# A fused vision tower on one core: the value product of each four tiles is issued one slot later

## The chip, the cores and the metric

The kernel runs on one core of a Trainium2 chip. The metric is the device time of one execution in microseconds (us); lower is better. TensorE (PE) multiplies matrices, ScalarE (ACT) applies functions such as exp, VectorE (DVE) reduces and adds, GpSimd (POOL) does small elementwise work, SyncE (SP) issues the transfers. Each engine runs its own instructions strictly in the order in which they were written, and waits at a semaphore until another engine has raised it.

## What is computed

A batch of 16 items of 1024 tokens of 64 features passes through a patch embedding, two attentions with 8 heads of 8 features, and two expert networks. Nearly all of the time goes into the attentions:

```python
qkv = (x @ qkv_w.T).reshape(B, N, 3, H, D).transpose(2, 0, 3, 1, 4)
q, k, v = (qkv[0], qkv[1], qkv[2])
attn = jnp.einsum('bhnd,bhmd->bhnm', q, k) * scale
attn = jax.nn.softmax(attn, axis=-1)
out = jnp.einsum('bhnm,bhmd->bhnd', attn, v)
```

N is 1024 and H is 8. The first attention adds a bias; between and after the attentions stand layer norms, projections, a two-layer routed network and a top-2 expert network with gelu.

## The kernel before

**Tiles and slots.** The scores of one item and one attention are cut into 128 tiles of 128 keys by 512 queries; with 16 items and two attentions there are 4096 tiles. The program runs through *slots*, one for each tile n. The attentions of two items are interleaved with everything else in a *pair* of 256 slots. There are 15 pairs, 12 of them in a loop, with a phase of 128 slots ahead and one behind. In what follows a slot is named by its number in the pair, 0 to 255.

**The work of a slot.** TensorE issues in slot n, in this order: the side stages put there by hand (layer norm transposes, projections, expert layers; these are all lines but the three named here); the *score product* of tile n (line 914, `scores`), which puts 128x512 scores into one of three PSUM banks, the ring; and a *natural product* (line 902, `nat`) for a tile 46 slots ahead, of which VectorE takes the row maxima (line 1322). ScalarE then turns the scores into `prob` with exp (line 1113), which frees the bank. Once in four slots comes the *value product* (line 928, `pv`): it multiplies `prob` of four tiles by the values, four heads side by side in the array, and adds them up in the bank `acc`.

**What a score product waits for.** The ring of three banks is planned at build time (`score_ring`). A tile normally gets the bank of the tile three before it, and so waits for exp(n-3). A side stage that needs a bank of the ring takes it and keeps it for four tiles (`SIDE_TILES`); during those four slots the tiles alternate between the other two banks, and tile n waits for exp(n-2). I call these *two-bank* slots. The plan has some 1300 of them, in runs of four, so that about 330 fall on each remainder of n by four. In slots with n % 4 of 0 or 1 that are two-bank, the natural product is issued ahead of the score product (`scores_first`); in all others the score product comes first.

**What the value product waits for.** `pv` of tiles 4k to 4k+3 waits for exp(4k+3), line 927. The first one of a half item also waits until ScalarE has copied the finished `acc` out (line 1094, `acc_out`, after the exp of each slot that is 2 modulo 64), and that copy in turn waits for the value product before. `prob` has 8 buffers; exp(4k) waits for the value product of tiles 4k-8 to 4k-5.

**The expert network.** In slot 50 of each pair stands `FW`: on TensorE eight steps of four products each (lines 855 and 857), and on ScalarE eight gelu of 128x1024 (line 1085) behind a load of its function table. Its first step waits for the mask, its second step for the exp of slot 49, and from the third step on TensorE and ScalarE take turns. The line 871 follows in slot 51.

Of the kernel before, what the change touches and what calls it, by code (L numbers as in the profile page):

```python
# [49 lines left out]
HEADS = 4  # L50
# [275 lines left out]
def super_of(kind, it, q):  # L326

    n = q // SUPERS
    if kind == "first":
        a, b = 0, n  # L330
    elif kind == "last":
        a, b = 1, B - 1 + n
    elif n == 0:
        a, b = 0, it + 1
    elif n == 1:
        a, b = 1, it
    else:
        a, b = (1, B - 1) if isinstance(it, int) and it == B - 2 else (0, it + 2)
    return a, b, q % 2, q % SUPERS // 2


def max_tiles(side, n):


    def extra(m):
        for slot in range(m, max(m - 3 * AHEAD, -1), -1):
            if any(x[0] == "FW" for x in side.get(slot, ())):
                return AHEAD - (m - slot) // 3
        return 0

    return range(n + SUPER + LEAD + (extra(n - 1) if n else 0), n + SUPER + LEAD + extra(n) + 1)


def before_phase(kind, it):

    if kind == "first":
        return None
    if kind == "last":
        return 1, B - 2
    return (0, 0) if isinstance(it, int) and it == 0 else (1, it - 1)  # L360


def tower_kernel(nc, x, w_dft, dft, const, onehot, qk_w, v_w, pw, qk_scale, wi, routed, shared, wo, bo,
                 table, route, wg, w1, b2, w2, out):
    with ExitStack() as ctx:
# [142 lines left out]
        def n_tiles(kind):  # L508

            return 2 * ATTN if kind == "pair" else ATTN  # L510
# [186 lines left out]
        def _(eng):  # L697
# [185 lines left out]
            def turn(n0, q, n):  # L883

                eng.wait_ge(parts_ready, over(n0, SUPER) + q + 1)
                eng.matmul(side_bank(n, 1)[:, 0:P], mpart[:, q % 2, :], ident_b[:, :], start=True, stop=True)\
                    .then_inc(side_full[1], 1)

            def nat(kind, it, n0, m):
                q, j = m // SUPER, m % SUPER  # L890
                a, b, g, half = super_of(kind, it, q)
                u = buffer_of(a, b)
                if q % SUPERS == 0 and j == 0:
                    if a == 0 and b < 2:
                        eng.wait_ge(s_rows[u], 2 * PARTS * 16)
                    eng.wait_ge(qk_in[u][0], at(DMA_QK * (loads_before(a, b) + 1)))
                if q % SUPERS == 1 and j == 0:
                    eng.wait_ge(qk_in[u][1], at(DMA_QK * (loads_before(a, b) + 1)))
                use = n0 + m
                eng.wait_ge(nat_free, at(use - len(NAT) + 1))  # L900
                h, c, kh = HEADS * g + j // 8, half * 512 + j % 8 // 2 * P, j % 2
                eng.matmul(NAT[use % len(NAT)][:, :], QA[u][0:K_NAT, h, c:c + P],  # L902
                           KA[u][0:K_NAT, h, kh * 512:kh * 512 + 512], start=True, stop=True)\
                    .then_inc(nat_ready, 1)

            def scores(kind, it, n0, n):
                q, i = n // SUPER, n % SUPER
                a, b, g, half = super_of(kind, it, q)
                u = buffer_of(a, b)
                if i == 0:  # L910
                    eng.wait_ge(maxrow_in[q % 2], at(DMA_MAX * (over(n0, 2 * SUPER) + q // 2 + 1)))
                bank_wait(TILE_PREV[n0 + n])
                t, h = i // HEADS, HEADS * g + i % HEADS
                eng.matmul(RING[TILE_BANK[n0 + n]][:, :], KA[u][0:K_ALL, h, t * P:t * P + P],  # L914
                           QA[u][0:K_ALL, h, half * 512:half * 512 + 512], start=True, stop=True)\
                    .then_inc(st_ready, 1)

            def pv(a, b, g, n0, first_tile):

                t = first_tile % SUPER // HEADS  # L920
                q = first_tile // SUPER
                if t == 0 and g == 0:
                    eng.wait_ge(acc_free, at(over(n0, 2 * SUPER) + q // 2))
                    if q % SUPERS == 0:
                        eng.wait_ge(vc_done, at(vc_index(a, b)))
                eng.wait_ge(exp_done, at(n0 + first_tile + HEADS))
                for hh in range(HEADS):
                    mm = eng.matmul(ACC[32 * hh:32 * hh + 32, :], VZ[buffer_of(a, b)][:, t, HEADS * g + hh, :],  # L928
                                    prob[:, (first_tile + hh) % TILES, :],
                                    start=(t == 0 and g == 0), stop=(t == JT - 1 and g == 1),  # L930
                                    skip_group_check=True)
                mm.then_inc(pv_done, 1)

            def body(kind, it, n0, side, found):
                if kind == "serial":
                    for k, stage in enumerate(side):
                        side_stage(stage, found[0, k], N_TILES, 0)
                    return
                if kind == "first":
                    eng.wait_ge(s_dve, SET_DVE)  # L940
                    eng.wait_ge(s_pool, SET_POOL)
                    for m in range(SUPER + LEAD):
                        if m == SUPER + LEAD - SUPER + TURN:
                            turn(n0, 0, found[-1, 0])
                        nat(kind, it, n0, m)
                for n in range(n_tiles(kind)):
                    if kind == "first" and n == LATE:
                        eng.wait_ge(s_rest, N_SET[s_rest])
                    tiles = max_tiles(side, n)
                    between = [(kind, it, n0, m) for m in tiles[:-1]]  # L950
                    for k, stage in enumerate(side[n]):
                        if stage[0] == "TN":
                            turn(n0, stage[1], found[n, k])
                        else:
                            side_stage(stage, found[n, k], n0 + n, n, between)
                    two_banks = TILE_PREV[n0 + n] == ("tile", n0 + n - 2)
                    scores_first = n % HEADS >= 2 or not two_banks
                    if scores_first:
                        scores(kind, it, n0, n)
                    for m in tiles[len(between):]:  # L960
                        if kind != "last" or m < ATTN:
                            nat(kind, it, n0, m)
                    if not scores_first:
                        scores(kind, it, n0, n)
                    if n % HEADS == 1 and n > 1:
                        done = n - 1 - HEADS
                        a, b, g, _ = super_of(kind, it, done // SUPER)
                        pv(a, b, g, n0, done)
                    elif n == 1 and kind != "first":
                        pv(*before_phase(kind, it), 1, n0, -HEADS)  # L970
                if kind == "last":
                    a, b, g, _ = super_of(kind, it, SUPERS - 1)
                    pv(a, b, g, n0, ATTN - HEADS)

            run_phases(eng, reg, body)


# [607 lines left out]
```

## Time and profile before

| what | value |
|---|---|
| median of 3 runs | 3964.97 us (3964.28 to 3965.2) |
| the profiled execution | 3963.26 us |
| its span, first to last instruction | 3961.5 us |
| mean granted TensorE clock | 0.985 of full speed |
| TensorE busy | 3796.0 us, 96% |
| VectorE busy | 2913.7 us, 74% |
| ScalarE busy | 2588.0 us, 65% |
| GpSimd busy | 873.0 us, 22% |

A matmul is shown as busy until its result has drained, some 0.38 us for 512 columns, while the next one starts after 0.22 us. So a wait of TensorE shows as idle time only for the part beyond that overlap, and the distance from start to start of two rows tells more than the busy share.

### The profile page before, as it was taken

What the parts mean: (1) busy time and instruction counts of PE and PEld (TensorE: products, weight loads), DVE (VectorE), ACT (ScalarE), POOL (GpSimd) and SP (SyncE); (2) the same over time, 40 slices, a digit from 0 to 9 for tenths busy, and PEclk for the clock granted to TensorE, in tenths of its full rate; (3) what the DMA queues carried; (4) which work ended last, traced back from release to release, by engine and by line L of the source; (5) the groups of instructions that cost most, each with busy time, mean ns of one, the idle gap of its engine ahead of it and who ended that gap; (6) DMA issues with size and microseconds to landing.
All of it is one profiled execution on the core that took longest, in us unless ns stands there. A gap on an engine that the chain in (4) does not pass through costs nothing.

```text
span 3961.5 us, 62513 instructions
## 1 busy us (share of the span) xinstructions
PE 3796.0 (96%) x21508; PEld 1325.7 (33%) x21508; DVE 2913.7 (74%) x5001; ACT 2588.0 (65%) x4720; POOL 873.0 (22%) x1265
## 2 busy tenths in 40 slices
PE   6999999999999999999999999999999999999896
PEld 3233333333333333333333333333333333333332
DVE  4877868677786877868677786877868678787672
ACT  0566667666676666766667676676666667677564
POOL 4122212132221312212122121312212122121211
PEclk7899999999999999999999999999999999999998
DMA  5213201212121122201212112122211222111100
GB/s 108 40 26 67 44 20 33 59 37 44 35 43 38 33 47 49 43 22 33 57 39 44 32 42 42 33 47 49 39 26 33 55 41 44 31 30 33 21 13 6
DMA packets 119068, 156.37 MB, mean 39 GB/s; under 512 B 24847, under 2 KB 66575, under 8 KB 118717
## 3 DMA queue, kind: packets, MB, share of 16 engines
q1 hardware_dynamic: 118753, 152.38, 19.2%
q8 instruction: 172, 2.82, 0.3%
q14 instruction: 143, 1.17, 0.1%
HBM read 120.01 MB, written 29.36 MB: 38 GB/s over the span
## 4 chain that ended last, share of the span: by engine, by line
PE 83%; ACT 5%; DVE 5%; issue 4%; SPq 1%; POOL 1%; DMA 1%; DVEq 0%; ACTq 0%; POOLq 0%
PE acc L928 24%; PE side_st L914 22%; PE nat L902 19%; PE side_st L871 3%; PE side_st L765 3%; DVE tile_max L1322 2%; PE side_st L855 2%; PE side_st L742 2%; ACT prob L1113 2%; PE side_st L822 2%; ACT hidden L1085 1%; PE side_st L787 1%; SPq L540 1%; PE side_st L780 1%; PE side_st L829 1%
## 5 line engine op out<-in xcount | busy, mean ns | idle before, releaser
L1322 DVE TENSOR_REDUCE tile_max<-nat 128x1 f32<-128x512 f32 x4096 | 2585.3, 683 | 904.8 <-PE nat L902 865.1
L1113 ACT ACTIVATE prob<-side_st 128x512 f32<-128x512 f32 x4096 | 2206.4, 600 | 1229.3 <-PE side_st L914 1196.1
L914 PE MATMUL side_st<-q_rows,k_rows 99*128 99x512 bf16 x4096 | 1555.0, 383 | 21.6 <-ACT prob L1113 15.9
L902 PE MATMUL nat<-k_rows,q_rows 96*128 96x512 bf16 x4096 | 1533.1, 384 | 26.3 <-DVE tile_max L1322 19.6
L928 PE MATMUL acc<-prob,v_padded 128*32 128x512 f32 x8192 | 1093.6, 606 | 30.4 <-ACT prob L1113 29.4
L914 PEld LDWEIGHTS side_st<-q_rows,k_rows 99*128 99x128 bf16 x4096 | 397.3, 98 | 1197.6 <-ACT prob L1113 860.3
L902 PEld LDWEIGHTS nat<-k_rows,q_rows 96*128 96x128 bf16 x4096 | 399.8, 98 | 506.3 <-DVE tile_max L1322 269.8
L1487 POOL TENSOR_SCALAR max_parts<-neg_max 128x16 bf16<-128x16 f32 x128 | 26.5, 207 | 1750.4 <-DVE neg_max L1329 1750.2
L928 PEld LDWEIGHTS acc<-prob,v_padded 128*32 128x32 f32 x8192 | 162.2, 108 | 390.6 <-ACT prob L1113 229.4
L1412 POOL TENSOR_SCALAR ln_s<-ln_s 128x8 f32<-128x8 f32 x64 | 13.0, 203 | 697.9 <-DVE ln_s L1214 696.0
L1085 ACT ACTIVATE hidden<-side_st,b 128x1024 f32<-128x1024 f32 x128 | 139.0, 1113 | 18.7 <-PE side_st L857 18.5
L855 PE MATMUL side_st<-ln_rows,w 64*128 64x512 f32 x512 | 139.7, 623 | 5.9 <-ACTq L1074 1.3
L765 PE MATMUL side_st<-x_rows,w_patch 128*128 128x512 f32 x248 | 118.7, 623 | 8.9 <-DMA x_rows<-in_x 8.9
L871 PE MATMUL side_st<-hidden,w 128*64 128x512 f32 x512 | 113.4, 595 | 0.0
L1424 POOL TENSOR_TENSOR ln_s<-ln_s,const 128x8 f32<-128x8 f32 x64 | 105.6, 1650 | 11.8 <-POOL ln_s L1421 11.8
L765 PEld LDWEIGHTS side_st<-x_rows,w_patch 128*128 128x128 f32 x248 | 47.8, 199 | 71.5 <-issue 59.7
L1434 POOL TENSOR_TENSOR hidden<-hidden 128x1024 f32<-128x1024 f32 x32 | 68.2, 2130 | 5.9 <-POOL hidden L1432 5.9
L1438 POOL TENSOR_TENSOR hidden<-hidden 128x1024 bf16<-128x1024 f32 x32 | 68.1, 2129 | 5.9 <-POOL hidden L1436 5.9
L822 PE MATMUL side_st<-hidden,group_weights 128*128 128x256 f32 x256 | 69.4, 393 | 0.0
L1426 POOL TENSOR_TENSOR centred<-centred,ln_s 128x512 f32<-128x512 f32 x64 | 66.7, 1043 | 11.4 <-POOL ln_s L1424 11.4
L1417 POOL TENSOR_TENSOR squares<-centred 128x512 f32<-128x512 f32 x64 | 66.6, 1041 | 11.7 <-POOL centred L1415 11.7
L855 PEld LDWEIGHTS side_st<-ln_rows,w 64*128 64x128 f32 x512 | 41.5, 187 | 73.2 <-ACT hidden L1085 52.9
(126 smaller groups left out, 2002.0 us busy)
## 6 DMA issues: line engine op xcount, KB each, us to landing
q_rows<-q_scratch SPq DMA_DIRECT2D x576, 64.0 KB
k_rows<-k_scratch SPq DMA_DIRECT2D x192, 192.0 KB
x_rows<-in_x SPq DMA_DIRECT2D x62, 512.0 KB, 6.4
q_scratch<-hidden SPq DMA_DIRECT2D x32, 384.0 KB
k_scratch<-hidden SPq DMA_DIRECT2D x96, 128.0 KB
group_weights<-in_routed SPq DMA_DIRECT2D x64, 129.0 KB, 2.1
q_rows<-max_rows SPq DMA_DIRECT2D x512, 3.0 KB
out_h<-out_rows SPq DMA_DIRECT2D x16, 256.0 KB, 2.1
```

Source lines behind the costliest of these rows:

```text
L742: mm = eng.matmul(both[par][:, j * cols:j * cols + cols], rows[half, j * P:j * P + P], w[half, :], start=(j == 0), stop=True, skip_group_c ...
L765: mm = eng.matmul(bk[:, :], Wf[:, j, :, :].rearrange("p a o -> p (a o)"), xv[:, :, j, :], start=(j == 0), stop=(j == 3))
L822: mm = eng.matmul(bk[:, c:c + 256], WC[:, g, ll, 0:HID], HE[:, ll, g * 256:g * 256 + 256], start=(g % 2 == 0), stop=True, skip_group_check ...
L855: eng.matmul(both[par][:, :], W1[half, e, :], XT[half, :], start=True, stop=False)
L871: mm = eng.matmul(SIDE[0][half, :], w, m, start=(e < 0), stop=(e == E - 1), skip_group_check=True)
L902: eng.matmul(NAT[use % len(NAT)][:, :], QA[u][0:K_NAT, h, c:c + P], KA[u][0:K_NAT, h, kh * 512:kh * 512 + 512], start=True, stop=True)\
L914: eng.matmul(RING[TILE_BANK[n0 + n]][:, :], KA[u][0:K_ALL, h, t * P:t * P + P], QA[u][0:K_ALL, h, half * 512:half * 512 + 512], start=True ...
L928: mm = eng.matmul(ACC[32 * hh:32 * hh + 32, :], VZ[buffer_of(a, b)][:, t, HEADS * g + hh, :], prob[:, (first_tile + hh) % TILES, :], start ...
L1085: eng.activation(HE[:, e, :], both[:, :], ACT.Gelu, bias=b1[:, e:e + 1]).then_inc(he_ready, 1)
L1113: eng.activation(prob[:, n % TILES, :], RING[TILE_BANK[n0 + n]][:, :], ACT.Exp).then_inc(exp_done, 1)
L1322: eng.tensor_reduce(mx[:, q % 2, j // 8, j % 8 // 2, j % 2:j % 2 + 1], NAT[use % len(NAT)][:, :], AX.X, ALU.max).then_inc(nat_free, 1)
L1424: eng.tensor_tensor(ln_s[:, 4, :], ln_s[:, 3, :], half_pow, ALU.pow).then_inc(ln_p, 1)
```

## The change

The value product of tiles 4k to 4k+3 was issued at the end of slot 4k+5, the second slot of the next four. It is now issued at the end of slot 4k+6, the third. The same holds for the last four tiles of a phase, which are finished in the phase behind it.

```diff
-                    if n % HEADS == 1 and n > 1:
-                        done = n - 1 - HEADS
+                    if n % HEADS == 2 and n > 2:
+                        done = n - 2 - HEADS
                         a, b, g, _ = super_of(kind, it, done // SUPER)
                         pv(a, b, g, n0, done)
-                    elif n == 1 and kind != "first":
+                    elif n == 2 and kind != "first":
                         pv(*before_phase(kind, it), 1, n0, -HEADS)
```

No instruction is added or removed, and only TensorE's order changes; the orders of ScalarE, VectorE, GpSimd and SyncE are the same.

TensorE around slots 54 to 59 of a pair, before. L886 is a side stage that takes a bank of the ring in slot 55, so that slots 55 to 58 are two-bank; L880 is the output stage in slot 56:

```order
2271 L886 MATMUL side_st<-ident_b,max_parts 128x128
2272 L914 MATMUL side_st<-q_rows,k_rows 128x512
2273 L902 MATMUL nat<-k_rows,q_rows 128x512
2274 L880 MATMUL side_st<-const,y_sum 128x128 x4
2275 L914 MATMUL side_st<-q_rows,k_rows 128x512
2276 L902 MATMUL nat<-k_rows,q_rows 128x512
2277 L914 MATMUL side_st<-q_rows,k_rows 128x512
2278 L928 MATMUL acc<-prob,v_padded 32x512 x4
2279 L914 MATMUL side_st<-q_rows,k_rows 128x512
2280 L902 MATMUL nat<-k_rows,q_rows 128x512
```

The same place in the changed kernel:

```order
2204 L928 MATMUL acc<-prob,v_padded 32x512 x4
2205 L886 MATMUL side_st<-ident_b,max_parts 128x128
2206 L914 MATMUL side_st<-q_rows,k_rows 128x512
2207 L902 MATMUL nat<-k_rows,q_rows 128x512
2208 L880 MATMUL side_st<-const,y_sum 128x128 x4
2209 L914 MATMUL side_st<-q_rows,k_rows 128x512
2210 L902 MATMUL nat<-k_rows,q_rows 128x512
2211 L914 MATMUL side_st<-q_rows,k_rows 128x512 x2
2212 L902 MATMUL nat<-k_rows,q_rows 128x512
2213 L928 MATMUL acc<-prob,v_padded 32x512 x4
```

The score products of slots 57 and 58 now stand side by side (x2), where the value product stood between them; it follows one natural product later, and the one before it has moved to just ahead of L886.

TensorE around the expert network in slot 50, before: the score product of slot 49, the value product, and FW (L855, L857), whose last step is followed by slot 50's own products and by L871 of slot 51:

```order
2849 L914 MATMUL side_st<-q_rows,k_rows 128x512
2850 L928 MATMUL acc<-prob,v_padded 32x512 x4
2851 L855 MATMUL side_st<-ln_rows,w 128x512 x2
2852 L857 MATMUL side_st<-mask_rows,mask_far 128x512 x2
...
2867 L857 MATMUL side_st<-mask_rows,mask_far 128x512 x2
2868 L914 MATMUL side_st<-q_rows,k_rows 128x512
2869 L902 MATMUL nat<-k_rows,q_rows 128x512
2870 L871 MATMUL side_st<-attn_or_mask_rows,b 64x512 x2
```

And in the changed kernel:

```order
2765 L914 MATMUL side_st<-q_rows,k_rows 128x512
2766 L855 MATMUL side_st<-ln_rows,w 128x512 x2
2767 L857 MATMUL side_st<-mask_rows,mask_far 128x512 x2
...
2782 L857 MATMUL side_st<-mask_rows,mask_far 128x512 x2
2783 L914 MATMUL side_st<-q_rows,k_rows 128x512
2784 L902 MATMUL nat<-k_rows,q_rows 128x512
2785 L928 MATMUL acc<-prob,v_padded 32x512 x4
2786 L871 MATMUL side_st<-attn_or_mask_rows,b 64x512 x2
```

The value product has moved from ahead of the whole expert network to behind it.

## Rows read from the trace of the kernel before

**Rows 1.** The page: granted TensorE clock in 40 slices, in tenths (9: 90% or more).

```profile
PEclk7899999999999999999999999999999999999998
```

**Rows 2.** Busy time by stretch: window, length, five engines' busy us, clock, DMA.

```profile
1220.00:1460.00 240.00, 234.71 (x1338) 81.73 (x1334) 180.28 (x310) 162.95 (x297) 52.04 (x78) 1.00 0.20 40
```

**Rows 3.** Groups by line: busy us, mean ns of one, idle us before, what ended it.

```profile
L1113 ACT ACTIVATE prob<-side_st 128x512 f32<-128x512 f32 x4096 | 2206.4, 600 | 1229.3 <-PE side_st L914 1196.1 <-ACT ln_rows L1027 3.0 <-ACT hidden L1002 2.9
L914 PE MATMUL side_st<-q_rows,k_rows 99*128 99x512 bf16 x4096 | 1555.0, 383 | 21.6 <-ACT prob L1113 15.9 <-ACT hidden L1085 3.3 <-DMA q_rows<-max_rows 2.2
L928 PE MATMUL acc<-prob,v_padded 128*32 128x512 f32 x8192 | 1093.6, 606 | 30.4 <-ACT prob L1113 29.4
```

**Rows 4.** Timeline, TensorE, a cycle with three banks: start, length, line.

```profile
1007.09 0.38 PE L914 MATMUL side_st<-q_rows,k_rows 99*128 99x512 bf16 x1
1007.31 0.38 PE L902 MATMUL nat<-k_rows,q_rows 96*128 96x512 bf16 x1
1007.62 1.06 PE L928 MATMUL acc<-prob,v_padded 128*32 128x512 f32 x8
1008.62 0.39 PE L914 MATMUL side_st<-q_rows,k_rows 99*128 99x512 bf16 x1
```

**Rows 5.** Timeline, TensorE, slots 57 and 58 of the fifth pair, two banks.

```profile
1234.30 0.38 PE L914 MATMUL side_st<-q_rows,k_rows 99*128 99x512 bf16 x1
1234.61 1.06 PE L928 MATMUL acc<-prob,v_padded 128*32 128x512 f32 x8
1235.61 0.39 PE L914 MATMUL side_st<-q_rows,k_rows 99*128 99x512 bf16 x1
```

**Rows 6.** Timeline, ScalarE, the exps of slots 56, 57 and 58 there.

```profile
1234.28 1.08 ACT L1113 ACTIVATE prob<-side_st 128x512 f32<-128x512 f32 x2 [0.28 <-PE side_st L914]
1236.04 0.60 ACT L1113 ACTIVATE prob<-side_st 128x512 f32<-128x512 f32 x1 [0.67 <-PE side_st L914]
```

**Rows 7.** Timeline, TensorE: the score product of slot 25, two banks.

```profile
1189.02 0.38 PE L914 MATMUL side_st<-q_rows,k_rows 99*128 99x512 bf16 x1
```

**Rows 8.** Timeline, ScalarE: the exp of slot 24.

```profile
1188.84 0.60 ACT L1113 ACTIVATE prob<-side_st 128x512 f32<-128x512 f32 x1
```

**Rows 9.** Timeline, TensorE: the score product of slot 213, two banks.

```profile
1374.77 0.38 PE L914 MATMUL side_st<-q_rows,k_rows 99*128 99x512 bf16 x1
```

**Rows 10.** Timeline, ScalarE: a side evacuation, then the exps of slots 212, 213.

```profile
1374.59 0.77 ACT L1036 ACTIVATE hidden<-side_st,b_qk,qk_scale 128x512 f32<-128x512 f32 x1
1375.25 1.08 ACT L1113 ACTIVATE prob<-side_st 128x512 f32<-128x512 f32 x2
```

**Rows 11.** Timeline, TensorE, slot 49 and the first two steps of FW.

```profile
1208.78 0.38 PE L914 MATMUL side_st<-q_rows,k_rows 99*128 99x512 bf16 x1
...
1210.09 1.13 PE L855 MATMUL side_st<-ln_rows,w 64*128 64x512 f32 x4
...
1211.27 1.02 PE L855 MATMUL side_st<-ln_rows,w 64*128 64x512 f32 x4
```

**Rows 12.** Timeline, ScalarE: the exps of slots 48 and 49.

```profile
1209.75 1.08 ACT L1113 ACTIVATE prob<-side_st 128x512 f32<-128x512 f32 x2 [0.17 <-ACT mask_rows L1072]
```

**Rows 13.** Timeline, TensorE: the natural and value products of slot 69.

```profile
1242.40 0.38 PE L902 MATMUL nat<-k_rows,q_rows 96*128 96x512 bf16 x1
1243.01 1.07 PE L928 MATMUL acc<-prob,v_padded 128*32 128x512 f32 x8 [0.23 <-ACT prob L1113]
```

**Rows 14.** Timeline, ScalarE: `acc_out` in slot 66.

```profile
1241.78 0.59 ACT L1094 ACTIVATE acc_sb<-acc 128x512 f32<-128x512 f32 x1
```

**Rows 15.** Timeline, TensorE: score products of slots 175 and 177.

```profile
1340.81 0.38 PE L914 MATMUL side_st<-q_rows,k_rows 99*128 99x512 bf16 x1
...
1342.89 0.39 PE L914 MATMUL side_st<-q_rows,k_rows 99*128 99x512 bf16 x1 [0.74 <-ACT prob L1113]
```

**Rows 16.** Timeline, ScalarE, before it: a side evacuation, then exps from slot 175.

```profile
1341.29 0.83 ACT L1063 ACTIVATE hidden<-side_st,group_weights 128x256 f32<-128x256 f32 x2
1342.23 1.68 ACT L1113 ACTIVATE prob<-side_st 128x512 f32<-128x512 f32 x3
```

**Rows 17.** Timeline, TensorE: waits in slots 12/13, 40 and 149 of the pair.

```profile
1178.50 0.38 PE L902 MATMUL nat<-k_rows,q_rows 96*128 96x512 bf16 x1
1179.01 0.77 PE L742 MATMUL side_st<-w_proj,attn_or_mask_rows 64*128 64x64 f32 x9
...
1201.94 0.39 PE L902 MATMUL nat<-k_rows,q_rows 96*128 96x512 bf16 x1 [0.16 <-DVE tile_max L1322]
...
1318.19 0.39 PE L902 MATMUL nat<-k_rows,q_rows 96*128 96x512 bf16 x1 [0.53 <-DVE tile_max L1322]
```

## The prediction, made before the run

> **What bounds the kernel now.** I read the page first, then busy time by stretch, the groups by line, and the timelines of TensorE and ScalarE beside each other. In the steady stage TensorE is busy for 234.71 of 240 us at full clock [rows 1, 2]; VectorE with 180.28 and ScalarE with 162.95 us have room [rows 2]. One pair of 256 slots takes 238 us. The groups put nearly all of ScalarE's idle time, 1196.1 of 1229.3 us, down to waiting for score products, while these wait only 15.9 us for an exp and the value products 29.4 us [rows 3]. So TensorE's own order sets the time, and a wait put into it costs its full length.
>
> Four prices come from starts. After a natural or score product the next product starts 0.22 us later, a value product 0.31 us later, and what follows the value product 1.00 us after that [rows 4]. Taken out of its place, the value product thus makes room of 0.31 + 1.00 - 0.22 = 1.09 us; put back elsewhere it takes 1.09 us. An exp lasts 0.60 us [rows 3] and starts 0.43 us after its score product when ScalarE is free (1235.61 to 1236.04) [rows 5, 6]. The product that waited for an exp starts 0.06 us after its end: 1342.23 + 0.60 = 1342.83, and the row is at 1342.89 [rows 15, 16].
>
> **Three banks: nothing changes.** With three banks each score product waits for the exp three tiles back, and a cycle is four pairs of products and one value product, wherever in the four it stands. The fourth score product after a value product waits for the exp of the first: 0.43 + 0.60 + 0.06 = 1.09 us, against 3 x 0.44 = 1.31 us of products between them. No wait before, none after. The value product itself gets more slack than before.
>
> **Two banks: the value product was a cover.** The score product of slot 4k+2 waits there for exp(4k). Before, the value product stands ahead of it. Now the product ahead is that of slot 4k+1, and the exp is not done. Two-bank slots of this kind with no side stage in between are 16 in a pair. I read each from the trace as: end of exp(4k) + 0.06 - (start of the last product ahead of the value product + 0.22).
> - The common case is slot 58: 1234.28 + 0.60 + 0.06 = 1234.94, against 1234.30 + 0.22 = 1234.52, a wait of 0.42 us [rows 5, 6]. Eight places have it (slots 38, 58, 90, 134, 146, 186, 222, 250): 3.3 us.
> - Where TensorE already lost time just ahead to VectorE, the wait is smaller. Slot 26: 1188.84 + 0.66 = 1189.50, against 1189.02 + 0.22 = 1189.24, so 0.26 us [rows 7, 8]. Five places have 0.26 to 0.30 (26, 122, 154, 182, 218): 1.4 us.
> - Where ScalarE evacuates a side stage ahead of the exp, it is larger. Slot 214: line 1036 holds the exp of slot 212 back to 1375.25, so 1375.91 against 1374.99, 0.92 us [rows 9, 10]. Slots 130 and 170 have the same pattern with 0.83 us: 2.6 us.
>
> The value product then follows at full price, since nothing behind it waited for it in a way that gives the time back. Sum: 7.3 us a pair.
>
> **The expert network: the cover moves too.** Before, its first step starts at 1210.09 behind the value product and the second at 1211.27 [rows 11]. Now the second step waits for the exp of slot 49: that pair of exps ends at 1209.75 + 1.08 = 1210.83 [rows 12], so it starts at 1210.89, only 0.38 us earlier. From there on ScalarE's and TensorE's turns keep their lengths, so all moves up by 0.38. The value product costs 1.00 us behind slot 50's natural product (0.31 + 1.00, less the 0.31 that the fp32 side product needs there anyway, the price of its class that I take to be the value product's [rows 4]). Net 0.6 us a pair. Slots behind natural products with side stages (layer norm, embedding, transposes) wait for things done long before, so there I take nothing.
>
> **What comes back.** With the value product one slot later, waits just behind its old place are covered.
> - After `acc_out` (ending 1242.37) the exps run late and the value product of slot 69 starts 0.61 us after its natural product instead of 0.31 [rows 13, 14]. At its new place that exp is done. `acc_out` itself now waits for the value product of its own slot: it starts about 0.2 us before the next exp could, delaying that by some 0.2 us, within the 0.22 us slack of the three-bank case. Two places a pair: -0.6 us.
> - The score product of slot 177 starts at 1342.89, since its exp stood behind line 1063 and a late score product [rows 15, 16]. If the value product is issued a slot later, in 174, then that slot's exp and line 1063 run during it. By the prices above slot 177's product starts 0.75 us earlier against the rest: -0.75 us.
> - Natural products that wait for VectorE: slot 40 (0.54 from 1201.40, that is 0.32 too much, and 0.15 more in slot 41) and slot 149 (0.69 too much here, 0.38 as a mean of the pairs); and the projection in slot 13, 0.51 after its natural product (at 1178.50) where 0.31 would do [rows 17]. A value product now stands between them and what they wait for: -0.47, -0.38, -0.20 us.
>
> Sum: -2.4 us a pair.
>
> **The sum.** 7.3 + 0.6 - 2.4 = 5.5 us a pair, times 15 pairs is 83 us; the phases at both ends have too few such places to count. The profiled execution took 3963.3 us, so 4046 us, and the median lies 1.7 us above that execution: 4048 us.
>
> The page TensorE: Matmul & The Clock Gate of the Trainium skill, section Back-to-back issue gap, gives 131 ns as the sustained spacing of 512-column products. The rows show 0.22 us, and I go by them. By the page the products ahead of the waiting one would end sooner and each common wait would be about 0.26 us longer (three products), some 4 us a pair more.
>
> **Rivals.**
> 1. *The waits do not come back.* If what I book as covered only moves on to the next product, the loss is 7.9 x 15 = 119 us: 4084 us. For it: two of the five entries rest on VectorE, which is busy for three quarters of the time. Against: the value product gives it 1 us at just that point. Chance 0.10.
> 2. *The other side: the value product's wait is the one that counts.* Value products wait 29.4 us for exps [rows 3]. If the two-bank score products had their banks in time, only the regained waits would be left: -2.4 x 15 = -36 us, 3929 us. It decides once the waits in front of slots 4k+2 stay under 0.15 us each (2.4 over 16). Against it speaks that the exp of slot 56 ends at 1234.88, which no order of TensorE's makes earlier. Chance 0.03.
> 3. *Waits and gains cancel*: within 8 us of 3965, with half the loss and a doubled gain. Chance 0.03.
> 4. *The clock falls.* The stage ran at 1.00 [rows 2], with TensorE idle for moments of up to 0.74 us [rows 15]. More such moments could take the clock to its lower level of 1.2 GHz for stretches. If it cost 5% of the stage, as an estimate from the slices at the start with a digit of 8 [rows 1], the time would be near 4160 us. TensorE: Matmul & The Clock Gate of the Trainium skill, section A second HAM failure mode: psum-queue depth-cycling, tells of a kernel in which short idle moments between groups of products made the clock swing; by it this would be the outcome here, while the trace has such moments at full clock throughout. Chance 0.02.
>
> That the change does nothing is excluded by the order: the value product of every group has moved.
>
> **How the numbers follow.** My forecast, a loss of some 5.5 us a pair, has 0.82: 4048 us. Its own bounds come from the regained part, which may be between half and one and a half times 2.4: 6.7 or 4.3 us a pair, so 4030 to 4066 us. For 8 times in 10 I stretch it up to near rival 1 and down by as much: 4012 to 4080 us. About 0.2%, 8 us, is what a measurement of this kernel can tell from no change. Faster 0.03, within 0.02, slower 0.95.
>
> **What would show it.** In the profile after: idle time of line 914 ended by exp grows from 15.9 us to some 70 to 90 us (a wait of 0.42 us shows as about 0.26, since 0.16 us of a product's length is overlap); that of line 928 falls from 29.4 to a few us. In a two-bank group the product of slot 4k+2 starts 0.42 us later than 0.22 after its forerunner; FW's second step starts about 2.1 us after slot 49's score product instead of 2.5; three-bank cycles keep 2.84 us; a pair takes 243 to 244 us; the clock stays at 1.00. I would be wrong if the pair grew by under 3 us or over 8, or if line 928 still waited.

## The result and the profile after

The changed kernel takes 4040.81 us as the median of 4 runs (4037.32 to 4045.07), against 3964.62 us (3962.12 to 3965.2) for the kernel before. The ratio is 1.0197, with a 95% interval of 1.0185 to 1.0208: slower by 76 us. The forecast was 4048 us, range 4012 to 4080 us. The profiled execution took 4043.53 us with a span of 4041.8 us, 80.3 us more than that of before.

The groups by line after (busy us, mean ns of one, idle us before and what ended it), which answer to [rows 3]; the fourth is the expert network's first product:

```profile
L1113 ACT ACTIVATE prob<-side_st 128x512 f32<-128x512 f32 x4096 | 2207.2, 600 | 1268.6 <-PE side_st L914 1237.6
L914 PE MATMUL side_st<-q_rows,k_rows 99*128 99x512 bf16 x4096 | 1551.1, 384 | 89.7 <-ACT prob L1113 82.4
L928 PE MATMUL acc<-prob,v_padded 128*32 128x512 f32 x8192 | 1095.6, 607 | 0.7 <-ACT prob L1113 0.7
...
L855 PE MATMUL side_st<-ln_rows,w 64*128 64x512 f32 x512 | 141.6, 630 | 15.3 <-ACTq L1074 10.6
```

The exp, the score product and the value product last as long as before. What changed is who waits. The score product's idle time behind an exp has grown from 15.9 to 82.4 us, and the value product's has gone from 29.4 to 0.7 us. In this stretch the clock did not move; it is the one of [rows 2], at full clock:

```profile
1220.00:1460.00 240.00, 231.22 (x1313) 79.43 (x1312) 177.41 (x306) 160.34 (x291) 49.11 (x76) 1.00 0.20 39
```

In the same 240 us TensorE got through 1313 matmuls instead of 1338. The waits of TensorE (line, releaser: us in total, times, the longest):

```profile
PE side_st L914 <- ACT prob L1113: 82.4, 248, 0.8
PE side_st L780 <- POOL centred L1426: 23.4, 6, 9.4
PE nat L902 <- DVE tile_max L1322: 21.2, 37, 5.1
PE side_st L803 <- DVEq L1256: 16.9, 32, 1.5
PE side_st L855 <- ACTq L1074: 10.6, 16, 1.3
```

**The common case** is slots 57 and 58 of the fifth pair, first TensorE, then ScalarE in the same stretch (start, length, what), to be read beside [rows 5, 6]:

```profile
1261.46 0.38 PE L914 MATMUL side_st<-q_rows,k_rows 99*128 99x512 bf16 x1
1262.09 0.39 PE L914 MATMUL side_st<-q_rows,k_rows 99*128 99x512 bf16 x1 [0.25 <-ACT prob L1113]
1262.32 0.38 PE L902 MATMUL nat<-k_rows,q_rows 96*128 96x512 bf16 x1
1262.63 1.06 PE L928 MATMUL acc<-prob,v_padded 128*32 128x512 f32 x8
```

```profile
1261.44 1.08 ACT L1113 ACTIVATE prob<-side_st 128x512 f32<-128x512 f32 x2 [0.28 <-PE side_st L914]
```

The two score products stand side by side, and the second starts 0.63 us after the first instead of 0.22. It starts 0.05 us after the end of the exp of slot 56 (1261.44 + 0.60 = 1262.04). The wait of 0.41 us shows as 0.25 us of idle time, since a product counts as busy for 0.38 us. **The large case**, slots 213 and 214, with ScalarE behind it, answers to [rows 9, 10]:

```profile
1403.38 0.38 PE L914 MATMUL side_st<-q_rows,k_rows 99*128 99x512 bf16 x1
1404.52 0.39 PE L914 MATMUL side_st<-q_rows,k_rows 99*128 99x512 bf16 x1 [0.76 <-ACT prob L1113]
```

```profile
1403.20 0.77 ACT L1036 ACTIVATE hidden<-side_st,b_qk,qk_scale 128x512 f32<-128x512 f32 x1
1403.87 1.08 ACT L1113 ACTIVATE prob<-side_st 128x512 f32<-128x512 f32 x2
```

The second product starts 1.14 us after the first, which is a wait of 0.92 us: the evacuation in line 1036 holds the exp back.

**Place by place.** The middle pairs run through the same plan, so the two traces can be laid over each other. For each four slots I took the time from the score product two slots ahead of the value product's old slot to the one two slots behind it, in both kernels, and the difference, as a mean of the 12 middle pairs (they agree within 0.02 us at most places). The places are named by the old slot of the value product.

| places | forecast, us a pair | measured, us a pair |
|---|---|---|
| eight common two-bank places (37, 57, 89, 133, 145, 185, 221, 249) | 3.3 | 0.42+0.42+0.39+0.47+0.41+0.41+0.42+0.39 = 3.3 |
| five small ones (25, 121, 153, 181, 217) | 1.4 | 0.24+0.31+0.12+0.17+0.28 = 1.1 |
| three large ones (129, 169, 213) | 2.6 | 0.82+0.83+0.92 = 2.6 |
| expert network (49) | 0.6 | 0.65 |
| behind `acc_out` (69, 197) | -0.6 | -0.27-0.27 = -0.5 |
| slot 177 | -0.75 | -1.00 |
| natural products (41, 149), projection (13) | -1.05 | -0.26-0.25-0.20 = -0.7 |
| not in the forecast: 101, 109 | 0 | -0.87+0.75 = -0.1 |
| not in the forecast: 9, 21, 117, 113 | 0 | 0.30+0.27+0.23-0.14 = 0.7 |
| not in the forecast: 209 | 0 | -0.52 |
| the rest, each under 0.2 | 0 | -0.6 |
| sum | 5.5 | 4.8 |

13 pairs at 4.8 us, the first with 7.7 and the last with 5.5, make 75.5 us. The rest of the 80.3 us lies outside the pairs: the stretch ahead of them was 3.8 us longer, and that behind them 0.9 us. The stretch ahead says nothing of the change: it takes between 213.1 and 219.5 us in the thirteen traces, in no order that follows the place of the value product. The first pair has another plan than the middle ones (no expert network, for one), and in both kernels part of it ran at the clock's lower level of 1.2 GHz, behind waits of TensorE for GpSimd and VectorE (the longest 1.89 us, and 1.42 us before). The granted clock from 236 to 258 us was 0.61, where it was 0.84 before. How much of the first pair's 2.9 us above the 4.8 comes from that, and whether the change brought it on, no run separates.

### The profile page after: what moved, and what is told of

It reads as the page before. It is cut to its first block, busy times and chain, and to the rows that moved or that the text cites. A ratio compares the mean times of both kernels' runs of the same rounds, so it can differ in the third digit from the quotient of the medians.

```text
span 4041.8 us, 62513 instructions
## 1 busy us (share of the span) xinstructions
PE 3819.4 (94%) x21508; PEld 1314.0 (33%) x21508; DVE 2920.9 (72%) x5001; ACT 2596.6 (64%) x4720; POOL 871.5 (22%) x1265
## 4 chain that ended last, share of the span: by engine, by line
PE 79%; ACT 7%; DVE 6%; issue 4%; SPq 1%; POOL 1%; DMA 1%; POOLq 0%; DVEq 0%; ACTq 0%
PE acc L928 23%; PE side_st L914 21%; PE nat L902 18%; ACT prob L1113 4%; DVE tile_max L1322 4%; PE side_st L871 3%; PE side_st L765 2%; PE side_st L855 2%; PE side_st L742 2%; PE side_st L822 1%; ACT hidden L1085 1%; PE side_st L787 1%; SPq L540 1%; PE side_st L780 1%; PE side_st L772 1%
## 5 line engine op out<-in xcount | busy, mean ns | idle before, releaser
L914 PE MATMUL side_st<-q_rows,k_rows 99*128 99x512 bf16 x4096 | 1551.1, 384 | 89.7 <-ACT prob L1113 82.4
L855 PE MATMUL side_st<-ln_rows,w 64*128 64x512 f32 x512 | 141.6, 630 | 15.3 <-ACTq L1074 10.6
L1085 ACT ACTIVATE hidden<-side_st,b 128x1024 f32<-128x1024 f32 x128 | 139.0, 1113 | 20.1 <-PE side_st L857 19.9
L871 PE MATMUL side_st<-hidden,w 128*64 128x512 f32 x512 | 113.4, 595 | 0.0
L855 PEld LDWEIGHTS side_st<-ln_rows,w 64*128 64x128 f32 x512 | 40.7, 188 | 76.8 <-ACT hidden L1085 51.3
```

Source lines behind the costliest of these rows:

```text
L855: eng.matmul(both[par][:, :], W1[half, e, :], XT[half, :], start=True, stop=False)
L871: mm = eng.matmul(SIDE[0][half, :], w, m, start=(e < 0), stop=(e == E - 1), skip_group_check=True)
L1085: eng.activation(HE[:, e, :], both[:, :], ACT.Gelu, bias=b1[:, e:e + 1]).then_inc(he_ready, 1)
```

## The experiments

My theory (*cover*) is this: between the score products of slots 4k+1 and 4k+2 the value product hid the wait of the latter for exp(4k), where only two banks of the ring are in use; moved away, it leaves the wait open. The first rival (*buffers*): a value product issued later frees its `prob` buffers later, and the exps are held back wherever it stands. The second rival (*the place itself*): the later place costs TensorE something at each group. For the experiments that choose among groups, a function `late` was put ahead of `super_of`; lines of these kernels are 16 or 18 further down, so 914, 928 and 1113 read as 930, 944 and 1131.

**1. Late everywhere but over two-bank waits and the expert network.**

```diff
+def uncovered(slot, n0, side):
+    return TILE_PREV[n0 + slot + 1] == ("tile", n0 + slot - 1) and not any(
+        x[0] in SIDE_BANKS or x[0][:2] in ("FW", "FY") for x in side[slot + 1])
...
+def late(slot, n0, side):
+    return not uncovered(slot, n0, side) and not feeds_experts(slot, side)
...
+                    slot = n - (n % HEADS == 2)
+                    if slot % HEADS == 1 and n == slot + late(slot, n0, side):
```

`feeds_experts` is true where the next slot holds FW.

> The value product moves a slot later everywhere except where the next slot is two-bank with no TensorE side stage in it (271 groups, 18 places in a pair) and ahead of the expert network. Cover theory: the 16 places that showed waits cost 7.0 us and the expert network 0.65 us a pair in the changed kernel's trace; without them its 4.8 us a pair become about -2.2 us (some 0.7 us of regained waits hang on the moves that are left out), so 15 x -2.2 = -33 us against before: about 3932 us. Buffer rival (every later value product holds the prob buffers longer and delays the exps, wherever it stands): the loss goes with the number of late groups, 45 of 64, so about 4018 us.

Measured: 3942.28 us as the median of 5 runs, a ratio to before of 0.9947 (0.9933 to 0.996), faster than the kernel before. The middle pairs lie 1.95 us under before, where -2.2 was expected. The median is 10 us above the 3932 expected; the profiled run (3935.57 us, mean clock 0.985) is close to it, the four others have a mean clock of 0.982 to 0.984 and took 3938 to 3946 us. The place of slot 57 is back as it was, and no score product waits there:

```profile
1228.59 0.38 PE L930 MATMUL side_st<-q_rows,k_rows 99*128 99x512 bf16 x1
1228.90 1.06 PE L944 MATMUL acc<-prob,v_padded 128*32 128x512 f32 x8
1229.90 0.39 PE L930 MATMUL side_st<-q_rows,k_rows 99*128 99x512 bf16 x1
```

The two groups in that kernel:

```profile
L930 PE MATMUL side_st<-q_rows,k_rows 99*128 99x512 bf16 x4096 | 1552.0, 383 | 12.8 <-ACT prob L1131 6.2
...
L944 PE MATMUL acc<-prob,v_padded 128*32 128x512 f32 x8192 | 1096.1, 607 | 0.7 <-ACT prob L1131 0.7
```

Both kinds of wait are gone. 45 of 64 groups are late here and the kernel is faster: both rivals had wanted a loss.

**2. Late only over two-bank waits.** `late` returns `uncovered(slot, n0, side)`.

> Only the 271 groups in front of two-bank slots without a side stage move a slot later, all others stay as before. Cover theory: +7.0 us a pair less some 0.7 us regained behind them, so 15 x 6.3 = +95 us: about 4060 us, slower than the full change. Buffer rival: 18 of 64 groups, so about 3986 us.

Measured: 4050.53 us in one run, before 3963.77 us beside it. A middle pair is 6.2 us longer. With 271 of 1024 groups moved the kernel is slower than with all of them moved. The 16 places of the prediction show the same waits as in the full change within 0.01 us for most (slot 57: 0.41, 129: 0.82, 213: 0.92). The rule of the code finds 18 such places in a middle pair; at the other two, in front of slots 14 and 138, no wait opens (0.22 us from start to start). The value products keep their own waits:

```profile
L930 PE MATMUL side_st<-q_rows,k_rows 99*128 99x512 bf16 x4096 | 1550.4, 383 | 91.0 <-ACT prob L1131 80.2
...
L944 PE MATMUL acc<-prob,v_padded 128*32 128x512 f32 x8192 | 1092.1, 605 | 30.5 <-ACT prob L1131 29.7
```

It also says where the regained VectorE waits come from. Those at slots 41 and 149 are here (-0.41 and -0.35 us), although the value products of these two slots stay in their old place, and they are missing in experiment 1 (+0.16 each), where they move. They hang on the moves of slots 37 and 145: there a wait of 0.41 us opens, TensorE comes later by that much to the natural products that wait for VectorE, and their wait shrinks by nearly as much. So the cover of these two places was worth almost nothing. The natural product of slot 40 in the fifth pair, first in experiment 1, where it starts 0.54 us after its score product (1195.59) as in the kernel before, then here, where it starts 0.28 us after it (1228.47):

```profile
1196.13 0.39 PE L918 MATMUL nat<-k_rows,q_rows 96*128 96x512 bf16 x1 [0.17 <-DVE tile_max L1340]
```

```profile
1228.75 0.39 PE L918 MATMUL nat<-k_rows,q_rows 96*128 96x512 bf16 x1
```

The three parts add up: 6.19 here, 0.69 in experiment 3, -1.95 in experiment 1 make 4.93 us a pair, and the whole change 4.80.

**3. Late only ahead of the expert network.** `late` returns `feeds_experts(slot, side)`.

> Only the value product ahead of the expert network moves, 16 groups in all. Cover theory: 0.65 us each (1.00 us behind slot 50, 0.38 us won ahead of the second step), +10 us: 3975 us. Rival (ScalarE's gelu and table loads hide it, since TensorE waits there for them): 3965 us.

Measured: 3972.3 us in one run, 0.65 us at slot 49 in the middle pairs, 0.69 in all. (There are 15 such groups and not 16: the first pair has no expert network.) The rival is out. The changed kernel shows how: TensorE around slot 49, the end of slot 50, and ScalarE's exps of slots 48 and 49, which answer to [rows 11, 12]:

```profile
1235.18 0.38 PE L914 MATMUL side_st<-q_rows,k_rows 99*128 99x512 bf16 x1
1236.18 1.13 PE L855 MATMUL side_st<-ln_rows,w 64*128 64x512 f32 x4 [0.62 <-ACTq L1074]
...
1237.39 1.13 PE L855 MATMUL side_st<-ln_rows,w 64*128 64x512 f32 x4
```

```profile
1248.12 0.38 PE L902 MATMUL nat<-k_rows,q_rows 96*128 96x512 bf16 x1
1248.43 1.07 PE L928 MATMUL acc<-prob,v_padded 128*32 128x512 f32 x8
1249.43 0.65 PE L871 MATMUL side_st<-attn_or_mask_rows,b 64*64 64x512 f32 x2
```

```profile
1236.25 1.09 ACT L1113 ACTIVATE prob<-side_st 128x512 f32<-128x512 f32 x2 [0.17 <-ACT mask_rows L1072]
```

The first step now waits for the mask, the second starts 0.05 us after the exp of slot 49 (1237.34), 2.21 us after slot 49's score product where it was 2.49 before. So 0.28 of the 1.3 us that the value product had taken ahead of it are won for the second step (0.38 was forecast), and it takes 1.31 us behind slot 50, 1.00 more than the side product alone. For the network as a whole, from slot 49's score product to slot 50's, 0.23 us are won in the full change, and 0.11 us are won just ahead, at a natural product of slot 48. In this experiment, where the value products ahead keep their place, it is 0.35 us. Either way 0.65 us remain.

**4. and 5. More `prob` buffers.** The exp's wait is moved back by one group, with 12 and with 16 buffers:

```diff
-TILES = 8
+TILES = 16
...
-                        eng.wait_ge(pv_done, at(over(n0 + n - HEADS, HEADS)))
+                        eng.wait_ge(pv_done, at(over(n0 + n - 2 * HEADS, HEADS)))
```

> The changed kernel with 12 prob buffers instead of 8, and the exp's wait for the value product moved back by one group, so that a late value product can't hold an exp back. Cover theory: no exp waited for a buffer, so as the changed kernel, about 4041 us. Buffer rival: the loss goes, about 3965 us.

> As the run with 12 buffers, with 16 of them, so that each group finds its own tiles again over the phases' ends: the changed kernel with the exp's wait for the value product moved back by one group. Cover theory: about 4041 us. Buffer rival: about 3965 us.

Measured: 4041.63 and 4039.39 us, one run each. With 12 buffers, which don't divide the 128 and 256 slots of a phase, the group at a phase's end reads other buffers than its exps wrote, so that part of the computation is changed; with 16 it is not. Place by place both lie within 0.015 us of the changed kernel, 4.8 us a pair. The waits with 16 buffers:

```profile
PE side_st L914 <- ACT prob L1113: 82.5, 248, 0.8
```

These are the same 248 waits. The buffers play no part.

**6. and 7. A shorter exp, with the old and the new place.**

```diff
-                    eng.activation(prob[:, n % TILES, :], RING[TILE_BANK[n0 + n]][:, :], ACT.Exp).then_inc(exp_done, 1)
+                    width = 512 if n0 + n < TILES else 256
+                    eng.activation(prob[:, n % TILES, 0:width], RING[TILE_BANK[n0 + n]][:, 0:width],
+                                   ACT.Exp).then_inc(exp_done, 1)
```

> The kernel before with the exp on 256 of 512 columns of each tile but the first eight; the other half of prob stays old, so the output is not the reference's. TensorE sets the time, so little falls away: only the waits at slots 69, 177, 197 and 209, some 1.5 us a pair; about 3940 us.

> The changed kernel with the same short exp. Cover theory: the exp is some 0.2 us shorter, so each of the 16 waits in front of two-bank slots shrinks by that: slot 58 from 0.42 to about 0.2 us, slot 214 from 0.92 to about 0.7, the five small ones to about 0.05; the change then costs some 2 to 3 us a pair against the short-exp kernel before, 30 to 45 us in all. Rival (the later place costs in itself, through the array's order or the buffers): still 4.8 us a pair, 76 us.

Measured: 3922.72 us with the old place (3940 was expected; the short exp takes 2.6 us a pair off the waits and not 1.5) and 3959.98 us with the new one. The exp's group with the old place (line 1114 in these two kernels; with the new place it differs by 2.5 us in all):

```profile
L1114 ACT ACTIVATE prob<-side_st 128x256 f32<-128x256 f32 (+1 forms) x4096 | 1536.5, 384 | 1846.6 <-PE side_st L914 1710.4
```

An exp takes 384 ns instead of 600. The change now costs 37.3 us, 2.65 us a pair, instead of 76. The wait in front of slot 58 is 0.20 us where it was 0.42, in front of slot 214 it is 0.50 where it was 0.92, so it shrinks by the 0.22 us of one exp or, where two shortened exps stand in the way (that of slot 211 ahead of the evacuation, that of slot 212 behind it), by some 0.4. The first has its rows, TensorE and ScalarE:

```profile
1235.03 0.81 PE L914 MATMUL side_st<-q_rows,k_rows 99*128 99x512 bf16 x2
1235.67 0.38 PE L902 MATMUL nat<-k_rows,q_rows 96*128 96x512 bf16 x1
```

```profile
1235.01 0.38 ACT L1114 ACTIVATE prob<-side_st 128x256 f32<-128x256 f32 x1 [0.49 <-PE side_st L914]
```

The exp of slot 56 ends at 1235.39, the product of slot 58 starts at 1235.44 (0.22 ahead of the natural product), 0.41 after that of slot 57 instead of 0.63. A cost of the place itself would have stayed.

**8. Late only where it gains.** `late` returns `n0 % 256 == ATTN and slot in (65, 69, 97, 101, 173, 177, 197, 205, 209)`.

> The kernel before with the value product a slot later only in slots 65, 69, 97, 101, 173, 177, 197, 205 and 209 of each pair, where the traces of the changed kernel and of the cover-kept one gained. Their rows give -0.27 (69), -0.09 (97), -0.87 (101), -0.09 and -1.00 (173, 177), -0.27 (197), -0.04 and -0.52 (205, 209): -3.1 us a pair if none depends on the moves left out, 15 x -3.1 = -47 us, about 3917 us. Rival (the gain of slot 101 is only lent, and comes back as VectorE's wait at slot 109, 0.75 us): -2.4 us a pair, about 3928 us.

Measured: 3923.71 us as the median (3920.7 to 3928.09), ratio 0.9902 (0.9885 to 0.9918). This beats both kernels: 1% under before and nearly 3% under the changed one. The rival is out. A pair gains 2.85 us of the 3.1 expected: slot 101 its 0.87 without giving 0.75 back at slot 109, 177 its 1.00, 209 its 0.52, 69 its 0.27. Slot 197 gains nothing, though the same move had brought 0.27 in the full change. TensorE from slot 197 on, and ScalarE just before:

```profile
1348.32 0.38 PE L930 MATMUL side_st<-q_rows,k_rows 99*128 99x512 bf16 x1
1348.54 0.38 PE L918 MATMUL nat<-k_rows,q_rows 96*128 96x512 bf16 x1
1349.06 0.39 PE L930 MATMUL side_st<-q_rows,k_rows 99*128 99x512 bf16 x1
```

```profile
1347.92 0.59 ACT L1112 ACTIVATE acc_sb<-acc 128x512 f32<-128x512 f32 x1
1348.39 1.59 ACT L1131 ACTIVATE prob<-side_st 128x512 f32<-128x512 f32 x3
```

The score product of slot 198 waits there for the exp of slot 195 (1348.39 + 0.60), 0.52 us after its forerunner, as the value product had waited before. The wait was only passed on.

**9. The pairs around the copy of `acc`.** `late` returns `n0 % 256 == ATTN and slot in (69, 193, 197)`.

> The kernel before with only the value products of slots 69, 193 and 197 of each pair a slot later. Two readings of the wait after the copy of acc: (a) moving the value product of slot 69 or 197 alone only passes the wait on to the score product behind it, as at slot 198 of the run before; what gains is that the value product of slot 193 moves too, so that the copy starts later and stands at another place among the exps. Then slot 197 gains 0.27 us and slot 69 nothing: -4 us in all. (b) The move of slot 69 or 197 itself gains: both gain 0.27, -8 us.

Measured: 3961.66 us against 3962.3 us beside it, no difference that one run can tell. The places say more: slot 69, moved alone, gains 0.00 us, and slot 197, moved with 193, gains 0.16. So reading (a) holds in kind: what brings the gain is the value product ahead of the copy. Its size is 0.16 and not 0.27 us, 0.08 a pair in all. The full change keeps no more of it: there slot 197 gains 0.27 and slot 201 gives 0.11 back. In both kernels a natural product just ahead of a moved value product starts 0.11 us late (0.34 us after its score product in slot 198 here, 0.33 in slot 202 there, where 0.22 would do), each time 0.06 us after VectorE ends a `tile_max`, so 0.16 are left.

**10. and 11. Fewer two-bank slots.** `SIDE_TILES = 2` in place of 4, with the old and the new place.

> The kernel before with SIDE_TILES 2 instead of 4: the plan hands a side stage's ring bank back after two tiles, which leaves 668 two-bank slots in place of 1302, 82 instead of 327 of them with n % 4 of 2, and 33 instead of some 271 with no side stage in them. Score products may wait for side evacuations instead. A little slower or as before: 3960 to 3990 us.

> The changed kernel with SIDE_TILES 2. Cover theory: nearly no value product covers a two-bank wait any more, so the loss is gone but for a few places and the expert network (0.65 us a pair), while the gains at slots 69, 101, 177 and 209 stay: between -25 and +15 us against the same kernel with the old place. Rival (the later place costs in itself): +76 us.

Measured: 4137.04 us with the old place and 4124.68 us with the new. The base is 176 us slower than the 3961.39 us beside it, where I had expected 30 at most, since score products now wait for side evacuations. But on that base the change gains 12 us, 1.1 us a middle pair, instead of costing 76. The score and the value product with the old place:

```profile
L914 PE MATMUL side_st<-q_rows,k_rows 99*128 99x512 bf16 x4096 | 1559.8, 383 | 196.4 <-DVE max_rows L1315 73.2
...
L928 PE MATMUL acc<-prob,v_padded 128*32 128x512 f32 x8192 | 1095.8, 607 | 30.4 <-ACT prob L1113 29.4
```

And with the new one:

```profile
L914 PE MATMUL side_st<-q_rows,k_rows 99*128 99x512 bf16 x4096 | 1556.5, 384 | 192.3 <-DVE max_rows L1315 56.9
...
L928 PE MATMUL acc<-prob,v_padded 128*32 128x512 f32 x8192 | 1098.2, 608 | 0.7 <-ACT prob L1113 0.7
```

The value product's 29.4 us go to 0.7 as ever, and the score product's idle time no longer grows. A base that waits so much elsewhere can also absorb waits, so this pair of runs supports the theory less strictly than experiments 6 and 7.

## Why the prediction was right

**What bounds the kernel.** TensorE's order, as read from [rows 2, 3]: each of the waits put into it is found again in the time.

**The three-bank case.** No change was forecast and none is there: in 17 of the 28 cycles of a pair that hold no two-bank slot the two traces agree within 0.01 us, and where the others differ by more than 0.12 us, they are rows of the table. It is the value product's waits (29.4 us) that vanish, as said.

**The two-bank case.** The reading "end of the exp + 0.06 - start of the last product + 0.22" gave 7.3 us a pair and 7.0 came. (The prediction counted 16 places of this kind; there are 18, and the two left out show no wait.) The common and the large places are right to 0.05 us; two of the small ones (153 and 181) came out at 0.12 and 0.17 instead of 0.26 and 0.28, since the VectorE wait ahead of them, which the reading leaves in place, shrank.

**The expert network.** 0.62 was forecast and 0.65 measured. Moved alone (experiment 3), the product gives 0.35 us back ahead of slot 50, close to the 0.38 forecast.

**What comes back.** -2.4 was forecast and -2.25 measured, but not in the same parts, so that the sum is near is in part luck. Slot 177 gave more (-1.00). Slots 41 and 149 gave less (-0.51 against -0.85), and not for the reason given: I had written that the value product moved there covers the wait for VectorE. Where only it moves (experiment 1), nothing is gained; the gain comes from the waits that open at slots 38 and 146 just ahead (experiment 2). Of `acc_out` the size was nearly right (-0.5 against -0.6) and the reason wrong: I had written that at its new place the value product of slot 69 finds its exp done. It does, but experiment 9 shows that this alone passes the wait to the next score product.

**What was missing.** These are places for which I took nothing. The claim that side stages behind the old place wait for things done long before fails at slot 10, where the transpose of the attention's output waits for VectorE. TensorE there in the changed kernel:

```profile
1201.34 0.38 PE L914 MATMUL side_st<-q_rows,k_rows 99*128 99x512 bf16 x1
1201.96 0.63 PE L803 MATMUL side_st<-const,squares 128*128 128x128 f32 x4 [0.24 <-DVEq L1256]
```

The transpose starts 0.62 us after the score product where 0.22 to 0.31 would do. On the other side the value product at slot 101 had started 1.51 us after its natural product, a wait of 1.2 us behind ScalarE's evacuations (lines 999 to 1002), which I had not listed; before, TensorE there:

```profile
1273.84 0.38 PE L902 MATMUL nat<-k_rows,q_rows 96*128 96x512 bf16 x1
1275.35 1.06 PE L928 MATMUL acc<-prob,v_padded 128*32 128x512 f32 x8 [1.13 <-ACT prob L1113]
```

The same place after, and slot 109's part of the cycle behind it:

```profile
1301.42 0.38 PE L902 MATMUL nat<-k_rows,q_rows 96*128 96x512 bf16 x1
1301.87 0.39 PE L914 MATMUL side_st<-q_rows,k_rows 99*128 99x512 bf16 x1
```

```profile
1309.47 0.38 PE L914 MATMUL side_st<-q_rows,k_rows 99*128 99x512 bf16 x1
1310.44 0.39 PE L902 MATMUL nat<-k_rows,q_rows 96*128 96x512 bf16 x1 [0.58 <-DVE tile_max L1322]
```

Of 1.51 us from the natural product to the next one, 0.45 are left, and the gain is nearly all lost again two cycles on, where a natural product waits for VectorE. Experiment 8 leaves out the move of slots 105 and 109 and keeps the gain. All that was missing comes to about -0.6 us a pair, 9 us in all. The two-bank waits and the regained parts differ from the forecast by another 0.1 us a pair, and the first and the last pair add 3.5 us; together this puts the time some 7 us under the forecast.

**The rivals.** The first (waits do not come back) is out by the time, and the regained parts are seen one by one; in small it is true at slots 101 and 109. The second, a gain once the two-bank score products had their banks, did not come about here, but the kernels of experiments 1 and 8 are just that case: -1.95 and -2.85 us a pair, where -2.4 was named. The third, waits and gains that cancel, is out by the time (its chance, 0.03, stands as 0.02 in the closing line of the prediction; nothing hangs on it). As for the fourth, the granted clock was 1.00 over the twelve middle pairs of both traces, although the score product's idle time became four times as long in total. By that, the section A second HAM failure mode: psum-queue depth-cycling of TensorE: Matmul & The Clock Gate in the Trainium skill does not describe these pairs: in the whole trace 248 waits for an exp, 82.4 us in all and at most 0.8 us each, and in the middle pairs no swing of the clock. That does not hold for every kernel of this case. In experiment 10, where score products idle for 196.4 us in all, the clock did fall to 1.2 GHz in the middle pairs, if rarely: just behind two waits of 1.07 and 1.01 us it was 0.96 from 1340 to 1380 us, a value product there took 1.94 us instead of 1.06, and the pair took 251.4 us where its neighbours took 249.8:

```profile
1359.99 0.61 PE L914 MATMUL side_st<-q_rows,k_rows 99*128 99x512 bf16 x1 [1.01 <-DVE v_natural L1238]
...
1360.95 1.94 PE L928 MATMUL acc<-prob,v_padded 128*32 128x512 f32 x8
```

The spacing of 131 ns in the section Back-to-back issue gap of the same page of the Trainium skill is not seen either; it is 0.22 us here.

Two things were told wrongly ahead of the prediction: the 15 pairs are all written out one after the other, none of them stands in a loop, and the first of them has no expert network. The forecast took 15 pairs with one each; that is 0.6 us of its 83.

## What to carry to other kernels

On an engine that runs in order, long independent work between two dependent products is a cover: before it is moved, look for what it hides at each of its places, not only for what it waits for itself. A wait that opens just ahead of another wait costs little: at slots 38 and 146 nearly all of the 0.41 us came back at the next wait for VectorE. Where a plan gives some stretches fewer buffers, a fixed place in the cycle is right in one kind of stretch and wrong in the other, so choose it by place; here that turned a loss of 2% into a gain of 1%. A wait that vanishes from one instruction may stand at the next one on the same engine, and only start-to-start times of the whole cycle tell.

## What the runs showed of the hardware

The repetition is closer than I had expected: at most places the cost of the same move differs by 0.01 us between the middle pairs and between kernels, whereas whole executions of one kernel differ by up to 8 us. These differences go with the granted clock: the changed kernel took 4037.32 and 4038.08 us at a mean of 0.984, 4043.53 at 0.983 and 4045.07 at 0.982. In all traces but those of experiments 10 and 11 the clock's lower level lies outside the middle pairs: in the changed kernel the granted clock is 0.97 in the first pair and in the last one, and 1.00 over the twelve in the middle. An effect of 0.7 us a pair could thus be read from one trace each (experiment 3), which the times alone would barely show.
